# Four sets of expert buffers, and expert rows added to the output by accumulating indirect stores

## The chip, the cores and the metric

The kernel runs on one core of a Trainium2 chip. Its engines work side by side: TensorE (PE in the profile) multiplies, VectorE (DVE), ScalarE (ACT) and GpSimd (POOL) do the elementwise work, SyncE (SP) only issues transfers. Each engine runs its own list of instructions in order and waits on semaphores for the others. The metric is device time in microseconds (us) of one execution.

## The reference

A block of three parts on `x` of 64 sequences by 32 rows by 256 columns, 2048 tokens in all: cross attention to a context of 64 by 257 rows, causal self attention, and a mixture of experts. The change touches the last one.

```
x = x + xattn(layernorm(x), ctx)             # 16 heads, context of 257 rows per sequence
x = x + attn(layernorm(x))                   # causal, 32 rows, ternary weights
xt = layernorm(x)                            # 2048 tokens, 256 columns
probs = softmax(xt @ Wg)                     # 8 experts
eidx, gate = argmax(probs), its probability
pos  = how many earlier tokens chose the same expert
keep = pos < 256                             # an expert takes 256 tokens, the rest are dropped
xd[eidx*256 + pos] = xt                      # only kept tokens
oe = (silu(xd @ W1[e]) * (xd @ W3[e])) @ W2[e]         # 8 experts, hidden 352 (padded to 384)
out = oe[eidx*256 + pos] * gate * keep + (silu(xt @ sw1) * (xt @ sw3)) @ sw2
x = x + out
```

## The kernel before

The tokens are cut into 16 tiles of 128 rows (four sequences). The attention of a tile and the routing of the tile ahead of it are woven: each engine has a written list of steps (`START_ORDER` for the prologue, `ORDER` for a tile), and runs 15 full tiles with it. A 16th pass (`LAST`) runs only the steps named in `LATE`, in the order in which they stand in `ORDER`: the rest of the cross attention of the last four sequences (`pt3`, `o3`, `f`), self attention (`xt1` to `pr`), the second layer norm (`ln2`), the router's logits (`lg`), the shared expert (`up`, `dn`), the position of each token among its expert's tokens (`pos`), and `scat` on POOL, an indirect store of the 128 normalised rows to their slots in `expert_rows` in HBM. In `ORDER` the step `pos` stands behind `up` (on PE behind `dn` too). On DVE `pos` computes three things a token: the slot where it is written (`slot_s`), the slot where its result is read (`slots`), and its gate (`gates`). A tile's output without the experts (`base`) is stored to `out` by SP.

Then come the eight experts. For one expert PE turns the 256 rows (L898, `expert_turn`), does the 12 products of `W1` and `W3` (`expert_up`) and the 6 of `W2` (`expert_down`). A float32 product stands as two records in the trace, so an `up` is x24 and a `down` x12. ACT copies the turned rows (L942), takes the tanh (L1096), copies the result out of the PSUM bank `Db` to one of the two tiles `eo` (which lie in `o_halves`) and stores it to `expert_out` (L1104). DVE makes the hidden values (L1661, L1665). PE's order is skewed: `up` of expert e+1, `turn` of e+2, `down` of e. Weights (`ew13`, `ew2`), rows (`xd`) and `eo` have two sets each. SP asks for expert e+2's `W1`/`W3` (768 KB) and then its rows (256 KB) when PE has finished `up` of expert e, and for its `W2` when PE has finished `down` of e; all go into one queue.

When all eight results are in HBM, POOL gathers, for each of the 16 tiles, the result rows of its tokens (L1259, indirect loads into `got`), DVE multiplies by the gate and adds the base rows that SP has read back from `out` into `fin` (L1678), and SP stores four tiles at a time.

The lines of these steps are L554 to L585 (SP), L892 to L935 (PE), L1091 to L1117 (ACT), L1214 to L1260 (POOL) and L1609 to L1679 (DVE).

## Time and profile before

| | |
|---|---|
| time, median of 3 runs | 1506.91 us (1506.75 to 1508.54) |
| the profiled execution's own time | 1508.46 us |
| its span in the trace | 1506.6 us |
| PE / DVE / ACT / POOL busy | 86% / 66% / 56% / 35% |
| mean granted clock of TensorE | 0.933 of 2.4 GHz |
| tiles 1 to 15 and the prologue end, the last tile begins | about 1322 us |
| first expert's rows are turned on PE | 1385.97 us |
| last expert product ends | 1476.4 us |

Times in the trace run from the span's start; the span leaves 1.9 us of the profiled execution's time outside. A busy share is a mean over stages with different limits: up to about 1322 us PE is nearly full, after it the stages below have limits of their own, and they are read one by one.

### The profile page before, as it was taken

How to read it: one execution, taken by the hardware profiler on the slowest of the kernel's cores; microseconds unless marked ns; L12 is line 12 of the kernel's file. 1: busy time of each engine (PE TensorE's matmuls, PEld its weight loads, DVE VectorE, ACT ScalarE, POOL GpSimd, SP SyncE). 2: the span in 40 equal slices, each digit the busy share in tenths (PEclk: the TensorE clock that was granted, in tenths of full speed). 3: DMA queues.
4: the chain of work that ended last, by engine and by line, in shares of the span. 5: the costliest groups of instructions: out<-in, count | busy, mean ns of one | idle time of the engine just before them, and what ended most of it. 6: DMA issues, size and time to landing. Idle time of an engine off the chain costs nothing.

```text
span 1506.6 us, 35628 instructions
## 1 busy us (share of the span) xinstructions
PE 1297.3 (86%) x10526; PEld 874.2 (58%) x10526; DVE 987.6 (66%) x3748; ACT 837.5 (56%) x3560; POOL 531.6 (35%) x1337
## 2 busy tenths in 40 slices
PE   5877898999999999989898989899999999955881
PEld 2554565666666666665656656566666666634661
DVE  6754777777677777776767676777767777732212
ACT  4445575747475757566566657575747575711110
POOL 2044152525252533435352515252535243310004
PEclk9998999999999999999999999999999999876996
DMA  9000010101010100000000000010101011002344
GB/s 370 31 23 15 9 30 11 32 11 32 11 32 11 33 11 29 11 26 18 22 21 22 21 8 29 11 32 11 32 11 32 11 32 39 31 3 75 120 153 126
DMA packets 41191, 59.65 MB, mean 40 GB/s; under 512 B 5094, under 2 KB 35953, under 8 KB 40096
## 3 DMA queue, kind: packets, MB, share of 16 engines
q1 hardware_dynamic: 36880, 50.73, 10.6%
q0 software_dynamic: 2064, 6.14, 1.2%
q10 hardware_dynamic: 2176, 2.10, 0.4%
q14 instruction: 59, 0.48, 0.1%
q8 instruction: 12, 0.20, 0.1%
HBM read 48.62 MB, written 10.49 MB: 39 GB/s over the span
## 4 chain that ended last, share of the span: by engine, by line
PE 49%; DVE 21%; issue 9%; POOL 8%; DMA 3%; ACT 3%; POOLq 0%; DVEq 0%; SPq 0%; ACTq 0%
PE AB L594 25%; PE Db L594 9%; PE Eb L594 5%; POOL prob L1177 4%; PE C L719 4%; PE C L594 3%; DVE kst L1312 3%; DVE rq L1360 2%; DMA ctxn<-expert_rows 2%; DVE nc_ L1284 2%; DVE nc_ L1285 2%; DVE nb_ L1286 1%; PE C L787 1%; DVE prob L1471 1%; PE C L734 1%
## 5 line engine op out<-in xcount | busy, mean ns | idle before, releaser
L950 ACT ACTIVATE AB<-AB 128x128 f32<-128x128 f32 (+1 forms) x1160 | 305.3, 263 | 172.8 <-PE AB L594 168.3
L1132 POOL TENSOR_TENSOR pjunk<-pjunk 128x1 f32<-128x1 f32 x288 | 56.1, 195 | 748.4 <-DVE sinv L1482 431.3
L1312 DVE BATCH_NORM_STATS2 kst<-AB 128x6 f32<-128x256 f32 x512 | 181.8, 417 | 68.1 <-PE AB L594 63.0
L950 ACT ACTIVATION_READ_ACCUMULATOR AB<-AB 128x1 f32 (+1 forms) x1160 | 217.3, 187 | 0.0
L594 PE MATMUL AB<-wk_hi,c_hi 128*128 128x512 f16 x512 | 203.7, 398 | 11.9 <-DVE smax L1471 2.9
L594 PE MATMUL AB<-wk_lo,c_hi 128*128 128x512 f16 x512 | 201.3, 393 | 0.0
L594 PE MATMUL AB<-wk_hi,c_lo 128*128 128x512 f16 x512 | 199.7, 390 | 0.0
L1020 ACT ACTIVATE prob<-prob,nbias,rq 128x257 f32<-128x257 f32 x256 | 150.6, 592 | 7.9 <-DVE nbias L1477 7.9
L1177 POOL TENSOR_SCALAR prob<-prob,sinv 128x257 f32<-128x257 f32 x256 | 123.4, 482 | 20.2
L594 PE MATMUL AB<-ctxT,qpT 128*128 128x257 f32 x512 | 124.0, 385 | 0.0
L594 PEld LDWEIGHTS AB<-wk_hi,c_hi 128*128 128x128 f16 x512 | 52.2, 102 | 94.7 <-issue 25.2
L594 PE MATMUL Eb<-pT,cn_hi 128*128 128x512 f16 x256 | 88.3, 386 | 14.1 <-DVE o_halves L1492 7.5
L594 PEld LDWEIGHTS AB<-ctxT,qpT 128*128 128x128 f32 x512 | 92.3, 190 | 12.2 <-DVE smax L1471 0.2
L1014 ACT COPY rkb<-C 128x512 f32<-128x512 f32 x128 | 68.6, 591 | 54.2 <-PE C L719 53.3
L1471 DVE CUSTOM_DVE_ANT_0 prob<-AB,rkb 128x257 f32<-128x257 f32 x256 | 95.3, 421 | 0.0
L594 PEld LDWEIGHTS AB<-wk_hi,c_lo 128*128 128x128 f16 x512 | 51.9, 101 | 65.8 <-issue 9.6
L1487 DVE TENSOR_TENSOR pT<-C,pT 128x512 f16<-128x512 f32 x128 | 81.7, 679 | 11.1 <-ACT pT L989 10.4
L594 PE MATMUL Db<-wvo_hi,o_halves 128*128 128x256 f16 x512 | 86.5, 273 | 0.7 <-ACT o_halves L982 0.7
L594 PE MATMUL AB<-x_hi,wqk_hi 128*128 128x128 f16 x512 | 87.0, 219 | 0.0
L594 PE MATMUL AB<-x_lo,wqk_hi 128*128 128x128 f16 x512 | 87.0, 219 | 0.0
L594 PE MATMUL AB<-x_hi,wqk_lo 128*128 128x128 f16 x512 | 86.9, 219 | 0.0
L1492 DVE SCALAR_TENSOR_TENSOR o_halves<-Eb,o_halves 128x512 f16<-128x512 f32 x64 | 44.1, 690 | 64.0 <-ACT o_halves L982 64.0
(252 smaller groups left out, 2923.8 us busy)
## 6 DMA issues: line engine op xcount, KB each, us to landing
ctxT<-in_ctxT SPq DMA_DIRECT2D x64, 128.5 KB, 2.1
ctxn<-in_ctxn SPq DMA_DIRECT2D x64, 128.0 KB, 2.1
wq_hi<-in_w SPq DMA_DIRECT2D x4, 768.0 KB, 5.0
wq_lo<-in_w SPq DMA_DIRECT2D x4, 768.0 KB, 6.3
expert_rows<-base POOLq DMA_DIRECT2D x1, 2048.0 KB, 15.5
xin<-in_x SPq DMA_DIRECT2D x16, 128.0 KB, 2.2
prob<-in_wqT SPq DMA_DIRECT2D x1, 2048.0 KB, 20.4
xres<-in_x SPq DMA_DIRECT2D x16, 128.0 KB, 2.0
```

The costliest lines, as they stand in the source:

```text
L594: return pe.matmul(out, lhsT, rhs, start=start, stop=stop)
L719: ins = pe.transpose(C[:, n, KT * P * (g % 2) + P * tt:KT * P * (g % 2) + P * (tt + 1)], rkx[:, b % 2, tt, P * g:P * (g + 1)], ident)
L950: ins = nc.scalar.activation(k, k, ACT.Square, accum_out=sums[0:m, h:h + 1])
L1014: nc.scalar.copy(rkb[:, b % 2, 2 * n:2 * n + 2, 0:KT * P], C[:, n].rearrange("p (g n) -> p g n", g=2)).then_inc(drained[s].sem, 1)
L1020: ins = nc.scalar.activation(prob[:, b, g], prob[:, b, g], ACT.Exp, bias=nbias[:, b, g:g + 1], scale=rq[:, G * b + g:G * b + g + 1], accum ...
L1132: own.mark(pool.tensor_tensor(pjunk[:, 0:1], pjunk[:, 1:2], pjunk[:, 1:2], ALU.mult))
L1177: ins = pool.tensor_scalar(prob[:, b, g], prob[:, b, g], sinv[:, b, g:g + 1], P_SCALE, ALU.mult, ALU.mult)
L1284: step(V.scalar_tensor_tensor(c, w, -0.5, w, ALU.mult, ALU.mult))
L1312: ins = V.bn_stats(stats[:, 0, 2 * half + n], AB[0:m, 2 + half, 2 * D * n:2 * D * (n + 1)])
L1471: V.tensor_tensor_reduce(prob[:, b, g], AB[:, g, 0:SKV], rkb[:, b % 2, g], 1.0, BELOW, ALU.mult, ALU.max, smax[:, b, g:g + 1]).then_inc(dr ...
L1487: V.tensor_tensor(pT[:, b % 2, 1, tt], C[:, tt], pT[:, b % 2, 0, tt], ALU.subtract).then_inc(drained[s].sem, 1)
L1492: V.scalar_tensor_tensor(o_halves[:, 1, :, rows], Eb[:].rearrange("p (h q) -> p h q", q=SQ), 1.0 / P_SCALE, o_halves[:, 0, :, rows], ALU.m ...
```

## The change

1. Expert weights and rows get four sets instead of two. The new places are tiles that are free by then: `prob`, `wvo_hi`, `wvo_lo` and `qpT`. Weights of experts 2 and 3 are asked for in the last tile, their rows behind those of experts 0 and 1; experts 4 to 7 are asked for when experts 0 to 3 are through `up` and `down`. `eo`, the hidden values and the turned rows keep their number of sets.
2. The gather at the end is gone. A small table in HBM (`mark_rows`, in the place of `expert_out`) gets for each slot two words, the gate and the token's number. It is blanked in the prologue, filled by 16 indirect stores of 128 pieces of 8 bytes (`mark_tokens`), all in the last tile: three behind `n3`, twelve behind `ln1`, one behind `scat`. SP reads it back as `marks` in one transfer. ACT multiplies an expert's result by its slots' gates while copying it out of PSUM, and POOL adds it to `out` by two indirect stores of 128 rows an expert with `compute_op=ALU.add`; a slot without a token has an index out of bounds and is skipped. ACT may write `eo` again only when the stores of two experts earlier have landed.
3. In the prologue DVE works out each token's number for the table: one reduction and 16 small adds, between `ident16` and the split of `wk`, and a memset more.
4. The last tile has its own order (`LAST_ORDER`): `pos` ahead of `up` and `dn` on PE and DVE, `lg` ahead of `up` and `ph3` ahead of `tl3` on ACT.
5. The loops over the experts are written out.

```diff
+SETS = 4
+LAST_ORDER = {
+    "PE": "pt3 o3 f xt1 qkv qk sc pv st pr xt2 lg pos up dn".split(),
+    "ACT": "ph3 tl3 oh3 xt1 qkv qk sc pv xt2 lg up".split(),
+    "DVE": "dp3 do3 f qkv sc sm ys yv pr ln2 lg pos up dn".split(),
+    "POOL": "n3 mk0 ln1 mk1 y ln2 scat mk3".split(),
+}
...
@@ SP
+            for e in (0, 1):
+                load_up(e)
+                load_down(e)
+            store_base(p)
+            sp.wait_ge(filled["5"].sem, filled["5"].at(p, "pt2"))
+            load_up(2)
+            load_down(2)
+            sp.wait_ge(filled["D"].sem, filled["D"].at(LAST, "f"))
+            load_up(3)
+            load_down(3)
+            sp.wait_ge(scattered.sem, scattered.at(LAST, "scat"))
+            load_rows(0)
+            load_rows(1)
+            store_base(LAST)
+            sp.wait_ge(marked, 16 * TILES)
+            sp.dma_start(marks[:].rearrange("p e a two -> p (e a) two"), mark_rows.rearrange("(n p) two -> p n two", p=P))\
+                .then_inc(marks_in, 16)
+            load_rows(2)
+            load_rows(3)
+            for e in range(SETS, E):
+                p, k = Period("expert", (e - SETS) // 2), e % 2
+                sp.wait_ge(filled["2"].sem, filled["2"].at(p, f"h{k}"))
+                load_up(e)
+                load_rows(e)
+                sp.wait_ge(filled["D"].sem, filled["D"].at(p, f"dn{k}"))
+                load_down(e)
...
@@ ACT
-                act.wait_ge(oe_out[k].sem, oe_out[k].before(p))
-                drain(p, f"dn{k}", "D", flat2(eo[k]), Db[:])
-                act.wait_ge(drained["D"].sem, drained["D"].at(p, f"dn{k}"))
-                act.dma_start(oe_rows[bass.ds(i * (2 * CAP) + k * CAP, CAP), :].rearrange("(a p) c -> p a c", p=P), eo[k])\
-                    .then_inc(oe_out[k].sem, 16)
+                act.wait_ge(marks_in, 16)
+                if e >= 2:
+                    for a in range(2):
+                        act.wait_ge(res_out[k][a], 16 * (e // 2))
+                act.wait_ge(filled["D"].sem, filled["D"].at(p, f"dn{k}"))
+                for a in range(2):
+                    ins = nc.scalar.activation(eo[k][:, a], Db[:, DIM * a:DIM * (a + 1)], ACT.Copy, scale=marks[:, e, a, 0:1])
+                ins.then_inc(drained["D"].sem, 1)
...
@@ POOL
+            def mark_tokens(tiles):
+                if TILES - 1 not in tiles:
+                    pool.wait_ge(slot_ready.sem, slot_ready.before(LAST))
+                    pool.wait_ge(marks_blank, 16)
+                gate()
+                for n in tiles:
+                    pool.indirect_dma_start(mark_rows, bass.IndirectOffsetOnAxis(ap=slots[:, n:n + 1], axis=0), tile_marks[:, n], None,
+                                            bounds_check=E * CAP - 1, oob_is_err=False).then_inc(marked, 16)
...
-            for n in range(TILES):
-                pool.indirect_dma_start(got[n], None, oe_rows, bass.IndirectOffsetOnAxis(ap=slots[:, n:n + 1], axis=0))\
-                    .then_inc(gathered[n], 16)
+            pool.wait_ge(base_out.sem, base_out.at(LAST, "o"))
+            for e in range(E):
+                p, k = Period("expert", e // 2), e % 2
+                pool.wait_ge(drained["D"].sem, drained["D"].at(p, f"dn{k}"))
+                for a in range(2):
+                    pool.indirect_dma_start(d["out"], bass.IndirectOffsetOnAxis(ap=marks[:, e, a, 1:2].bitcast(U32), axis=0),
+                                            eo[k][:, a], None, bounds_check=TOKENS - 1, oob_is_err=False,
+                                            compute_op=ALU.add).then_inc(res_out[k][a], 16)
...
@@ DVE
+                step(V.tensor_reduce(token[:], tri, AX.X, ALU.add, negate=True))
+                for n in range(TILES):
+                    V.tensor_scalar(tile_marks[:, n, 1:2].bitcast(U32), token[:], float(P * n + P - 1), None, ALU.add)
...
-                here = fin[n // 4][:, n % 4]
-                V.scalar_tensor_tensor(here, got[n], gates[:, n:n + 1], here, ALU.mult, ALU.add)\
-                    .then_inc(res_ready, 1)
```

PE before, from the router's logits of the last tile (`wg`) to the first experts; `sw` is the shared expert, `onehot` and `seen` are the step `pos`:

```order
L594 MATMUL Db<-wg,xn2T 128x8 x2
L594 MATMUL C<-xn2T,sw 128x128 x12
L594 MATMUL Eb<-sw,hT 128x256 x3
L594 MATMUL Db<-onehot,consts_sb 128x8
L594 MATMUL Db<-seen,ones 128x8
L898 MATMUL Eb<-consts_sb,ctxn 128x128 x4
L594 MATMUL AB<-rkb,wq_hi 128x256 x12
L898 MATMUL Eb<-consts_sb,ctxn 128x128 x4
```

PE in the changed kernel at the same place:

```order
L614 MATMUL Db<-wg,xn2T 128x8 x2
L614 MATMUL Db<-onehot,consts_sb 128x8
L614 MATMUL Db<-seen,ones 128x8
L614 MATMUL C<-xn2T,sw 128x128 x12
L614 MATMUL Eb<-sw,hT 128x256 x3
L919 MATMUL Eb<-consts_sb,ctxn 128x128 x4
L614 MATMUL AB<-rkb,wq_hi 128x256 x12
L919 MATMUL Eb<-consts_sb,ctxn 128x128 x4
```

The two small products of `pos` moved ahead of the 15 products of the shared expert.

POOL before, from the last step `n3` (it ends with `plast`) to the end of the program:

```order
L1187 TENSOR_TENSOR plast<-prob,plast 128x4
L1152 TENSOR_TENSOR rstd<-var,minus_half 128x1 x3
L1132 TENSOR_TENSOR pjunk<-pjunk 128x1
L1218 DMA expert_rows<-xn,slot_s 2048x256
L1259 DMA pxT<-expert_out,slots 128x256 x8
L1259 DMA px<-expert_out,slots 128x256 x8
```

POOL in the changed kernel, the same stretch; `rstd` three times is `ln1`, `y` and `ln2`, `expert_out` now holds the table:

```order
L1199 TENSOR_TENSOR plast<-prob,plast 128x4
L1144 TENSOR_TENSOR pjunk<-pjunk 128x1
L1240 DMA expert_out<-tile_marks,slots 2048x2 x3
L1164 TENSOR_TENSOR rstd<-var,minus_half 128x1
L1144 TENSOR_TENSOR pjunk<-pjunk 128x1
L1240 DMA expert_out<-tile_marks,slots 2048x2 x12
L1164 TENSOR_TENSOR rstd<-var,minus_half 128x1 x2
L1144 TENSOR_TENSOR pjunk<-pjunk 128x1
L1230 DMA expert_rows<-xn,slot_s 2048x256
L1144 TENSOR_TENSOR pjunk<-pjunk 128x1
L1240 DMA expert_out<-tile_marks,slots 2048x2
L1286 DMA out<-o_halves,marks 2048x256 x16
```

Sixteen indirect stores stand between and behind the three `rstd`, and the 16 gathers at the end became 16 accumulating stores, two for each expert.

## Rows read from the trace of the kernel before

**Rows 1.** Waits, 1384 to 1480 us (total us, times, longest us).

```profile
PE Eb L898 <- DMA ctxn<-expert_rows: 20.5, 6, 7.2
```

**Rows 2.** PE in order of time, experts (start us, us, instructions, [idle before]).

```profile
1385.97 1.11 PE L898 MATMUL Eb<-consts_sb,ctxn 128*128 128x128 f32 x4 [7.19 <-DMA ctxn<-expert_rows]
1387.81 7.57 PE L594 MATMUL AB<-rkb,wq_hi 128*128 128x256 f32 x24 [0.72 <-issue]
1395.21 0.60 PE L898 MATMUL Eb<-consts_sb,ctxn 128*128 128x128 f32 x4
1396.57 5.44 PE L594 MATMUL AB<-rkb,wq_lo 128*128 128x256 f32 x24 [0.76 <-ACT rkb L942]
1401.85 0.60 PE L898 MATMUL Eb<-consts_sb,ctxn 128*128 128x128 f32 x4
...
1404.88 5.34 PE L594 MATMUL AB<-rkb,wq_hi 128*128 128x256 f32 x24
1413.60 1.12 PE L898 MATMUL Eb<-consts_sb,ctxn 128*128 128x128 f32 x4 [3.38 <-DMA ctxn<-expert_rows]
1414.51 5.21 PE L594 MATMUL Db<-wqk_lo,pT 128*128 128x256 f32 x12
...
1464.84 5.34 PE L594 MATMUL AB<-rkb,wq_lo 128*128 128x256 f32 x24
...
1473.59 2.83 PE L594 MATMUL Db<-wqk_lo,pT 128*128 128x256 f32 x12 [0.82 <-ACT o_halves L942]
```

**Rows 3.** Windows: length, PE, PEld, DVE, ACT, POOL busy, clock, DMA share, GB/s.

```profile
32.00:40.00 8.00, 5.17 (x13) 1.88 (x14) 7.62 (x24) 1.27 (x9) 0.00 (x0) 0.60 1.03 390
...
1376.00:1380.00 4.00, 2.06 (x12) 1.66 (x10) 1.89 (x12) 0.00 (x0) 0.00 (x1) 1.00 0.05 18
...
1384.00:1388.00 4.00, 1.31 (x5) 0.94 (x6) 0.00 (x0) 0.58 (x1) 0.00 (x0) 0.50 0.79 229
```

**Rows 4.** In order of time, the last tile's end, all engines.

```profile
1363.58 0.55 POOL L1152 TENSOR_TENSOR rstd<-var,minus_half 128x1 f32<-128x1 f32 x1 [24.87 <-DVE var L1572]
...
1371.54 4.62 PE L594 MATMUL C<-xn2T,sw 128*128 128x128 f32 x24
...
1372.85 0.23 DVE L1597 TENSOR_SCALAR onehot<-consts_sb,eidx 128x8 f32<-128x8 f32 x1
...
1378.41 0.37 PE L594 MATMUL Db<-seen,ones 128*128 128x8 f32 x2
...
1378.82 0.17 DVE L1613 CUSTOM_DVE_ANT_0 posx<-Db,onehot 128x8 f32<-128x8 f32 x1
...
1379.77 0.15 DVE L1624 TENSOR_TENSOR slot_s<-flat,lmax 128x1 uint32<-128x1 f32 x1
...
1380.73 1.11 POOL L1218 DMA_INDIRECT expert_rows<-xn,slot_s  x1 [0.54 <-issue]
1383.19 0.91 SPq L556 DMA_DIRECT2D ctxn<-expert_rows  x2
```

**Rows 5.** In order of time, the last tile's beginning.

```profile
1326.29 0.57 ACT L942 CAST pTl<-Db 12x512 f16<-12x512 f32 x1 [3.50 <-PE Db L594]
...
1327.48 0.59 PE L594 MATMUL Eb<-pT,cn_hi 128*128 128x512 f16 x1 [1.23 <-ACT pT L989]
...
1338.14 0.57 POOL L1152 TENSOR_TENSOR rstd<-var,minus_half 128x1 f32<-128x1 f32 x1 [13.36 <-DVE var L1297]
```

**Rows 6.** In order of time, the end of the program.

```profile
1476.51 0.58 ACT L942 COPY o_halves<-Db 128x512 f32<-128x512 f32 x1 [3.06 <-PE Db L594]
...
1480.13 1.00 POOL L1259 DMA_INDIRECT pxT<-expert_out,slots  x1 [98.29 <-DMA expert_out<-o_halves]
1481.44 0.96 POOL L1259 DMA_INDIRECT pxT<-expert_out,slots  x1 [0.30 <-issue]
...
1498.95 0.95 POOL L1259 DMA_INDIRECT px<-expert_out,slots  x1 [0.30 <-issue]
```

**Rows 7.** In order of time, PE's first product of the prologue.

```profile
12.08 0.61 PE L594 MATMUL AB<-wk_hi,y 128*64 128x512 f16 x1 [12.08 <-DVE wk_lo L1412]
```

More of the change, by code:

```diff
@@ L57 @@
 N_CONST = sum(CONSTS.values())
-DVE_STEPS = dict(pro=78, full=85, last=37, expert=0)
-POOL_STEPS = dict(pro=37, full=40, last=5, expert=0)
+DVE_STEPS = dict(pro=79, full=85, last=37, expert=0)
+POOL_STEPS = dict(pro=37, full=40, last=8, expert=0)
 class Period:
@@ L174, in steps_of @@
         return START_ORDER[engine]
+    if p.kind == "last" and engine in LAST_ORDER:
+        return LAST_ORDER[engine]
     return [s for s in ORDER[engine] if p.kind == "full" or s in LATE]
@@ L317, in build @@
         slots = sb("slots", [P, TILES], U32)
-        gates = sb("gates", [P, TILES])
+        tile_marks = sb("tile_marks", [P, TILES, 2])
+        token = sb("token", [P, 1])
+        marks = sb("marks", [P, E, 2, 2])
+        no_marks = sb("no_marks", [P, E * CAP // P, 2])
         sig = sb("sig", [P, FC, P])
@@ L572, in _ @@
-            with sp.Fori(0, E // 2 - 1) as i:
-                p = Period("expert", i)
-                for k in range(2):
-                    sp.wait_ge(filled["2"].sem, filled["2"].at(p, f"h{k}"))
-                    load_up(i * 2 + (2 + k), k)
-                    load_rows(i * 2 + (2 + k), k)
-                    sp.wait_ge(filled["D"].sem, filled["D"].at(p, f"dn{k}"))
-                    load_down(i * 2 + (2 + k), k)
-            for n in range(4):
-                sp.wait_ge(res_ready, 4 * n + 4)
-                sp.dma_start(d["out"][4 * n * P:4 * (n + 1) * P, :].rearrange("(a p) c -> p a c", p=P),
-                             fin[n]).then_inc(res_out, 16)
@@ L997, in wqk_high @@
                     .then_inc(hi_ready.sem, 1)
-            for k in range(2):
-                act.sem_inc(oe_out[k].sem, 16)
             def step_tw(p):
@@ L1238, in _ @@
                      "ln2": lambda p: rsqrt(p, "ln2", 3), "scat": scatter,
+                     "mk0": lambda p: mark_tokens(range(0, 3)), "mk1": lambda p: mark_tokens(range(3, TILES - 1)),
+                     "mk3": lambda p: mark_tokens([TILES - 1]),
                      "hl": step_hl, "rkl": step_rkl, "cl": split_last}
@@ L1364, in _ @@
             own.enter(PRO)
-            for tile_, value in ((zeros, 0.0), (ones, 1.0), (minus_half, -0.5), (seen, 0.0),
+            for tile_, value in ((zeros, 0.0), (ones, 1.0), (no_marks, NO_TOKEN), (minus_half, -0.5), (seen, 0.0),
                                  (heads, 0.0), (vals, 0.0), (plast, 0.0), (pTl, 0.0), (cl_rows, 0.0)):
```

165 lines of the change are left out of this document (70 added, 95 removed).

## The prediction, made before the changed kernel was run

> **What bounds the kernel now.** I read the engines' shares first, then the chain of waits over the last 250 us, the order of time from 1320 us to the end, and the windows for the clock. The page's mean PE share, 86%, belongs to the tiles; the change leaves these nearly as they are. What it touches are four stretches with other limits.
>
> In the experts PE is the engine that others wait for, and PE itself waits for rows: 20.5 us in 6 waits [rows 1]. 7.2 of them are the wait for the first rows, after the last slot is known. The other five, 13.3 us, come because an expert's rows stand in SP's queue behind 768 KB of weights of the same expert and are asked for only two experts ahead. Where rows are there, as between the third turn at 1401.85 and the third `up` at 1404.88 [rows 2], PE has no gap to speak of. The clock makes the waits dearer: PE had 1.00 of 2.4 GHz at 1376 to 1380 us, idled, and had 0.50 (1.2 GHz) at 1384 to 1388 [rows 3]. The first `up` then took 7.57 us where later ones take 5.34, and a `down` behind a wait took 5.21 where the last took 2.83 [rows 2].
>
> Before the experts a serial chain runs from the router to the first rows: one-hot, position, slot, store, load [rows 4]. After them the end is POOL's: 16 gathers, the first at 1480.13, the last at 1498.95, 1.25 us apart [rows 6]. PE's last product ended at 1476.4 [rows 2], so 30.2 us of the span of 1506.6 are tail.
>
> **The parts, with their sum.** All against the profiled execution.
>
> *Prologue, +1.7.* DVE's step `low` gets a reduction over 128 columns and 16 adds on one column, ahead of the split of `wk`; PE's first product waits for that split at 12.08 [rows 7]. From the first row of `pos` to `slot_s` DVE goes through nine such small instructions in 0.95 us, 0.106 each [rows 4], so 16 take 1.7; pipelined better they take 1.3, the reduction adds perhaps 0.3. I take 1.7. Later DVE is busy 7.62 of 8 us at 32 to 40 us [rows 3], so I count it as passed on in full. Bounds: 0, if the waits for weights there swallow it, and 2.7. The memset and the blanking of the table (one transfer nobody waits for until the last tile) cost nothing; cover for POOL's issue is PE's wait for DVE until 12.08.
>
> *`ph3` ahead of `tl3`, -1.0.* At the last tile's start ACT casts `pTl` (1326.29, 0.57 us) before `pT`, for which PE waits until 1327.48 [rows 5]. The `pT` banks are full before `Db` is, so up to 1.2 us go; at least 0.57 do, unless PE is then late for another half. I take 1.0.
>
> *Marks in the last tile, 0.* `mk0` issues three indirect stores and `mk1` twelve. Nearest rows: gathers follow each other every 1.25 us, the scatter takes 1.11 us to issue [rows 4, 6]. `mk0` then takes about 4.5 us with its gate, inside POOL's idle time of 13.36 us before `ln1` [rows 5]; `mk1` 12 x 1.25 + 0.7 = 15.7 us inside the 24.87 us before `y` [rows 4]. Behind the waiting POOL stand `y`, `ln2` and the scatter, and DVE and PE wait for each, so a thirteenth microsecond too many would go straight to the end: the point is 2.0 us a store. What nothing here shows is a store of pieces of 8 bytes. Lower bound 0, upper the rival below.
>
> In a sentence of its own: the Trainium skill, in DMA: Bandwidth & Descriptors (Specifications), says that pieces under 512 bytes make the transfer read, modify and write; no run here shows such pieces alone, and by that rule the table's stores could only be dearer than the 1 KB ones, which is the direction of that rival.
>
> *`pos` ahead of `up` and `dn`, -4.8.* The one-hot is ready at 1372.85 + 0.23 = 1373.08. PE's two small products ended at 1378.78 because 15 larger ones stood before them; now they may start at 1373.1 and, at half clock, end about 1373.95 instead of 1378.78 [rows 4]. Everything behind moves with them: slot at 1375.1 for 1379.92, scatter 1375.9 for 1380.73, SP's rows 1378.4 for 1383.19, first turn 1381.2 for 1385.97 [rows 2, 4]. PE's shared expert is moved back by 2.4 us: its products start at 1373.95 for 1371.54, and its last ends near 1380.9 by the same spacing, just ahead of the rows. So both are late at about the same time, and more than 4.8 is not to be had here. `mk3` adds 1.25 us on POOL behind the scatter, where nobody but the table waits.
>
> *First `turn` and `up` at full clock, -2.6.* PE now idles some 0.3 us before the first turn, not 7.19. From turn 1 to turn 2 took 9.24 us; with a row pair at full clock it is 1.36 (1395.21 to 1396.57) + 5.28 (to 1401.85) = 6.64 [rows 2]. Bounds: 0 and 2.6.
>
> *The experts, -18.2.* Rows 2 and 3 are asked for before the first product, the rest four experts ahead, so a period is 3.03 (turn to next `up`, 1401.85 to 1404.88) + 5.28 = 8.31 us. From the second turn: 6.64 + 5 x 8.31 + 3.03 + (1464.84 to the end 1476.42) 11.58 + 0.2 for two activations instead of one copy of `Db` = 63.0, against 81.2 in the trace [rows 2]. The check: 13.3 us of waits and nearly 5 us of half clock behind them. ACT and DVE have room in a period of 8.31. The stores, two an expert, need POOL for 2.5 us of 8.31, if one costs what a gather does.
>
> *The tail, -23.2.* From the last product: ACT 0.1 + 0.7 (two of 256 columns; one of 512 took 0.58), POOL's start 0.6 (the scatter's issue wait 0.54), the second store 1.25 later, landing 4.0, span end 0.3: 7.0 against 30.2 [rows 4, 6]. The scatter landed in 2.46 [rows 4]; the accumulating store also has to read `out`, and I take 4.0, bounds 2.5 and 8. POOL's price for issuing an accumulating store is nowhere in the trace: the nearest rows say 1.25, and I take that.
>
> The Trainium skill (DMA: Bandwidth & Descriptors, Rules for kernel authors) says an accumulate reads its destination and writes later, and under Latency gives about 0.8 us as the least HBM round trip; by that estimate a store lands after 2.46 + 0.8 = 3.3 us, and the sum is 0.7 lower.
>
> Sum: +1.7 - 1.0 - 4.8 - 2.6 - 18.2 - 23.2 = -48.1. Span 1458.5, the execution's own time 1508.46 - 48.1 = 1460.4. The median lies 1.55 under the profiled execution, so the prediction is **1458.8 us**.
>
> **Rivals.**
> *The table comes back late.* SP reads it as 2048 pieces of 8 bytes, and rows 2 and 3 stand behind it in the queue. Asked for at about 1382; the rows of experts 0 and 1, 512 pieces of 1 KB, had the first landing 2.8 us after issue (1383.19 to 1385.97) [rows 2, 4]. By the number of pieces the table could take 4 x 2.8 = 11 us or more; the third turn needs its rows at 1381.2 + 13.3 = 1394.5, so up to 12.5 us are free. At 20 us it would cost 7.5, and half clock behind it 2: 1468. For it: the piece count; against: the slack. 10%.
>
> *The mark stores hold POOL.* Past 2.0 us each, `y` is late. At 3 us: 12 x 3 + 0.7 - 24.9 = +11.8, so 1471 [rows 4]. Against: a gather has as many pieces and issues in 1.25. 7%.
>
> *The stores pace the experts.* `eo` has still two tiles: ACT waits for the stores of expert e-2 before it frees `Db`, and with ACT the tanh of the next expert stands, and PE. Two stores may take 8.31 us, 4.15 each. At 5 us each the run is theirs: the first store can start at 1381.2 + 17.2 = 1398.4, plus 0.7 for the earlier terms, 16 x 5 and 4.3 at the end give 1483. 10% for 4.2 to 6.4 us.
>
> *The same mechanism, on the other side.* The end passes 1506.6 when 1399.1 + 16 c + 4.3 does: from c = 6.45 us a store the kernel is slower than before; at 8 us it is 1531. For it speaks that no accumulating transfer is in the trace at all, and that they work on random rows of HBM; against, that a scatter of the same rows lands in 2.46 us [rows 4], and c would have to be over twice that. 5%.
>
> *The change doesn't do what it says.* PE still waits for rows, because weights of four experts share the queue, and only tail and `pos` gain: 1458.8 + 18.2 + 2 = 1479. Against: they are asked for 33 us ahead. 3%.
>
> **How the numbers follow.** The forecast has 65%, and its own range is 1452 to 1466: prologue 0 to 2.7, `ph3` 0 to 1.2, clock 0 to 2.6, landing 2.5 to 8, and some microseconds for code that is now written out instead of looped. The table late 10% (1462 to 1470), marks 7% (1465 to 1475), paced stores 10% (1466 to 1506), slow stores 5%, waits kept 3%. The range 1452 to 1478 holds the forecast and most of the first two rivals, and some of the third: 8 in 10. Faster by over 0.2% (about 3 us, what a measurement here can tell from no change) 94%, the same 1%, slower 5%.
>
> **What would show it.** Right: first turn on PE near 1382; no wait of PE for rows from then on; clock 1.00 throughout the experts; eight periods of 8.3 us; last product near 1451.5; two stores behind it, the end 7 us later; `rstd` of `y` not late. Wrong: POOL's accumulating stores more than 1.25 us apart, ACT's copies of `Db` released by a transfer instead of by PE, a third turn late behind the table, or POOL's `y` released by POOL itself. The forecast falls if the stores cost over 4.15 us each or the mark stores over 2.0.

## The result, and the profile after

| | before | changed kernel |
|---|---|---|
| median | 1506.83 us (1506.39 to 1508.54, 4 runs) | 1461.76 us (1457.33 to 1465.12, 4 runs) |
| profiled execution, its own time | 1508.46 us | 1458.61 us |
| its span | 1506.6 us | 1456.6 us |
| mean granted clock | 0.933 | 0.949 |

The ratio is 0.9697, 95% interval 0.9663 to 0.9731. In a second comparison the changed kernel had 1464.39 us (1462.32 to 1466.68, 4 runs) and 0.9707 (0.9681 to 0.9733). The forecast was 1458.8, with 1452 to 1466 as its own range.

The waits of the experts, total us, times, longest; this line answers to [rows 1]:

```profile
PE Eb L919 <- DMA ctxn<-expert_rows: 2.2, 1, 2.2
```

20.5 us in six waits have become 2.2 in one, and that one is the wait for the very first rows (3.1 in a second trace of the changed kernel). PE in order of time, in the places of [rows 2]:

```profile
1376.14 0.66 PE L919 MATMUL Eb<-consts_sb,ctxn 128*128 128x128 f32 x4 [2.22 <-DMA ctxn<-expert_rows]
1377.52 7.10 PE L614 MATMUL AB<-rkb,wq_hi 128*128 128x256 f32 x24 [0.72 <-issue]
1384.46 0.60 PE L919 MATMUL Eb<-consts_sb,ctxn 128*128 128x128 f32 x4
1385.79 5.42 PE L614 MATMUL AB<-rkb,wq_lo 128*128 128x256 f32 x24 [0.72 <-issue]
1391.04 0.60 PE L919 MATMUL Eb<-consts_sb,qpT 128*128 128x128 f32 x4
...
1394.07 5.34 PE L614 MATMUL AB<-rkb,prob 128*128 128x256 f32 x24
1399.25 0.60 PE L919 MATMUL Eb<-consts_sb,qpT 128*128 128x128 f32 x4
...
1444.15 2.83 PE L614 MATMUL Db<-wvo_lo,pT 128*128 128x256 f32 x12 [1.10 <-ACT o_halves L1123]
```

From the third turn at 1391.04 to the fourth at 1399.25 pass 8.21 us. Each later turn follows at that distance with no bracket behind it: the engine was never idle ahead of it. But the first `up` still takes 7.10 us instead of 5.3 to 5.4. The windows say why (length, PE, PEld, DVE, ACT, POOL busy, clock, DMA share, GB/s); they are the places of [rows 3] and those around the first turn:

```profile
1370.00:1372.00 2.00, 1.64 (x8) 1.35 (x7) 0.45 (x2) 0.00 (x0) 0.67 (x1) 0.60 0.46 31
1372.00:1374.00 2.00, 1.56 (x6) 1.06 (x6) 0.35 (x2) 0.00 (x0) 0.00 (x0) 1.00 0.81 134
1374.00:1376.00 2.00, 0.00 (x0) 0.00 (x0) 0.38 (x1) 0.00 (x0) 0.00 (x0) 1.00 0.47 136
1376.00:1378.00 2.00, 1.14 (x6) 0.91 (x7) 0.00 (x0) 0.58 (x1) 0.00 (x0) 1.00 0.84 68
1378.00:1380.00 2.00, 2.00 (x7) 1.61 (x7) 0.00 (x0) 0.00 (x0) 0.00 (x0) 0.60 0.79 241
1380.00:1382.00 2.00, 2.00 (x6) 1.59 (x6) 0.00 (x0) 0.00 (x0) 0.00 (x0) 0.54 0.00 0
...
1388.00:1446.00 58.00, 56.90 (x276) 49.81 (x275) 13.36 (x14) 15.05 (x27) 19.82 (x13) 1.00 0.49 114
```

PE stood idle in 1374 to 1376, and its clock then went to 0.60 and 0.54 until 1382. From 1388 to 1446 PE is busy 98% at 1.00 (2.4 GHz). The DMA columns hold something not foreseen: 46% busy at 31 GB/s in 1370 to 1372, 84% at 68 GB/s in 1376 to 1378. Pieces of 8 bytes were under way in both stretches: those of the last mark store in the first, those of the table on its way back in the second (2073 of the 2190 packets there are under 512 bytes). The last tile's end in order of time, all engines, answers to [rows 4]:

```profile
1355.74 0.57 POOL L1164 TENSOR_TENSOR rstd<-var,minus_half 128x1 f32<-128x1 f32 x1 [10.92 <-DVE var L1603]
...
1365.02 0.23 DVE L1628 TENSOR_SCALAR onehot<-consts_sb,eidx 128x8 f32<-128x8 f32 x1
...
1367.31 0.15 DVE L1655 TENSOR_TENSOR slot_s<-flat,lmax 128x1 uint32<-128x1 f32 x1
...
1368.25 1.03 POOL L1230 DMA_INDIRECT expert_rows<-xn,slot_s  x1 [0.52 <-issue]
...
1369.68 0.99 POOL L1240 DMA_INDIRECT expert_out<-tile_marks,slots  x1 [0.16 <-issue]
1370.62 0.90 SPq L572 DMA_DIRECT2D ctxn<-expert_rows  x2
...
1374.81 0.43 SPq L591 DMA_DIRECT2D marks<-expert_out  x1
```

POOL's `rstd` of `y` still had 10.92 us to spare: the marks did not hold it. The slot comes 2.29 us after the one-hot, where it came 6.92 after it. But SP asked for the first rows at 1370.62 and PE got them at 1376.14, 5.5 us later instead of 2.8, with the last tile's mark store (`mk3`, 1369.68) just ahead. The transfers, issue to landing, in the stretch 1369 to 1377:

```profile
ctxn<-expert_rows SPq DMA_DIRECT2D x2, 256.0 KB, 5.6
...
marks<-expert_out SPq DMA_DIRECT2D x1, 16.0 KB, 3.2
```

The table came back in 3.2 us and nobody waited for it. In the same stretch before, two such row loads took 2.9. The end of the program, in the place of [rows 6]:

```profile
1443.17 0.84 ACT L1123 ACTIVATE o_halves<-Db,marks 128x256 f32<-128x256 f32 x2 [4.45 <-PE Db L614]
...
1444.78 1.55 POOL L1286 DMA_INDIRECT out<-o_halves,marks  x1 [4.37 <-ACT o_halves L1123]
...
1447.10 0.84 ACT L1123 ACTIVATE o_halves<-Db,marks 128x256 f32<-128x256 f32 x2 [3.09 <-PE Db L614]
1448.71 1.55 POOL L1286 DMA_INDIRECT out<-o_halves,marks  x1 [0.53 <-issue]
1450.56 1.54 POOL L1286 DMA_INDIRECT out<-o_halves,marks  x1 [0.30 <-issue]
```

An accumulating store is issued in 1.55 us, 1.85 from one to the next, where a gather needed 1.25. Expert 6's second (at 1446.63) is still being issued when expert 7's result is there at 1447.94. The last product ends at 1446.98, so the tail is 9.6 us instead of 30.2. And the prologue's first product, answering to [rows 7], with the row of the adds ahead of it:

```profile
6.84 1.06 DVE L1433 TENSOR_SCALAR tile_marks<-token 128x1 uint32<-128x1 f32 x16
...
12.93 0.61 PE L614 MATMUL AB<-wk_hi,y 128*64 128x512 f16 x1 [12.93 <-DVE wk_lo L1443]
```

Where the 50.0 us between the two spans went, by milestones (`x` is the output of the cross attention, one a tile):

| stretch | before | after | difference | predicted |
|---|---|---|---|---|
| start to the first `x` | 147.3 | 143.8 | -3.5 | +1.7 |
| first to 15th `x` | 1112.8 | 1110.1 | -2.7 | 0 |
| 15th to last `x` | 76.64 | 73.54 | -3.1 | -1.0 |
| last `x` to `slot_s` | 43.0 | 39.9 | -3.1 | -4.8 |
| `slot_s` to the first turn | 6.2 | 8.8 | +2.6 | 0 |
| first turn to the second | 9.24 | 8.32 | -0.9 | -2.6 |
| second turn to the last product's end | 81.2 | 62.5 | -18.7 | -18.2 |
| last product's end to the end | 30.2 | 9.6 | -20.6 | -23.2 |

The sum is near the forecast's -48.1, but the terms are not all right: 10.0 us more than foreseen came in the first three rows, and 8.6 less in the four rows on `slot_s`, the first turn and the tail. Executions of one kernel differ by some microseconds in the first two rows (in the traces of the changed kernel's second run and of the kernel before alike, a stretch at half clock stands at about 34 us that the trace above has not: first `x` at 148.7 and 147.3), so these two rows are not read for one pair. The third row has a part of the clock in it as well: the mean granted clock of that stretch is 0.91 before and 0.95 after.

### The profile page after: what moved, and what is told of

Same layout as the page of the kernel before. It is cut to its first block, busy times and chain, and to the rows that moved or that the text cites. A ratio compares the mean times of both kernels' runs of the same rounds, so it can differ in the third digit from the quotient of the medians.

```text
span 1456.6 us, 35544 instructions
## 1 busy us (share of the span) xinstructions
PE 1286.4 (88%) x10526; PEld 868.3 (60%) x10526; DVE 982.2 (67%) x3750; ACT 839.7 (58%) x3568; POOL 558.5 (38%) x1357
## 3 DMA queue, kind: packets, MB, share of 16 engines
HBM read 44.44 MB, written 8.42 MB: 36 GB/s over the span
## 4 chain that ended last, share of the span: by engine, by line
PE 51%; DVE 21%; issue 9%; POOL 7%; ACT 3%; DMA 1%; POOLq 1%; DVEq 0%; ACTq 0%
PE AB L614 27%; PE Db L614 8%; PE Eb L614 6%; PE C L739 4%; POOL prob L1189 4%; PE C L614 3%; DVE kst L1340 3%; DVE rq L1388 2%; DVE nc_ L1312 2%; DVE nc_ L1313 2%; DVE nb_ L1314 1%; DVE prob L1502 1%; PE C L754 1%; PE C L807 1%; DVE px L1598 1%
```

## The experiments

**The changed kernel again.** No edit; it shows how far two comparisons agree and gives a second trace.

> The changed kernel again, to see how its executions spread: so far 1457.3, 1458.6, 1464.9 and 1465.1 us. If the two groups come from TensorE's clock before the last tile, an execution near 1465 has a granted mean near 0.944 and tiles 1 to 15 some 5 us longer than the 1110.1 us of the profiled one; the experts are then the same, first turn to last product 71 us. If they come from the stores at the end, the tiles agree within 1 us and the end is longer.

1464.39 us, ratio 0.9707. The profiled execution took 1466.7 us, 8.1 more than the first one. Neither of the two sources looked for holds these 8.1 us: the tiles took 1110.1 us again, and the tail is 9.6 us again. 4.9 lie ahead of the first `x` (148.7 for 143.8), 1.9 between the last `x` and the first turn, 1.3 between the first two turns (9.58 for 8.32; the first `up` took 8.12 us behind a wait of 3.10). With both traces at half clock in the same stretch of the prologue the first `x` came at 148.7 against 147.3 before: +1.4, near the +1.7 of the sum. The other traces below bear this out: where the mean clock up to the first `x` is 0.91, it comes at 147.1 and 147.3 in the two kernels without the 16 adds and at 148.4 and 148.7 in two with them; with the adds it comes at 146.5 to 146.9 where the clock is 0.92 and at 143.6 to 144.7 where it is 0.93. But from the last `x` to the one-hot, which the change does not touch on PE, DVE or ACT, it took 39.6 us where before took 36.1 and the first trace of the changed kernel 37.6. That is taken up below.

**Two sets instead of four.** Experts 0 and 1 loaded as before, the rest asked for two experts ahead; the accumulating stores stay.

```diff
-SETS = 4
+SETS = 2
...
-            load_up(2)
-            load_down(2)
...
-            load_up(3)
-            load_down(3)
...
-            load_rows(2)
-            load_rows(3)
```

> The changed kernel with SETS = 2: weights and rows of expert e+2 asked for, weights first, when expert e is through up, and no early loads of experts 2 and 3. Theory, the sets are worth what I summed for the experts: five or six waits of PE for rows of 2 to 3.4 us come back with half clock behind one or two of them, 15 to 18 us, 1477 to 1480. Rival, those waits came from the other traffic of the old end (the read-back of 2 MB of base rows, the result stores): under 4 us, at most 1466.

**Two sets, rows asked for ahead of the weights.**

```diff
+                load_rows(e)
                 load_up(e)
-                load_rows(e)
```

> The same with SETS = 2, but SP asks for the rows ahead of the weights. Theory, rows were late only because 768 KB stood before them in the queue: 256 KB land in 3 to 4 us, the turn comes 6.6 us after the asking and the weights are needed 8 us after it, so nearly all waits go, and two sets are as good as four within 3 us, near 1463. Rival, two sets are too few for the bytes: the wait moves to the weights (PE's up released by a transfer), and the time stays over 1470.

The first has 1475.47 us (0.9785, 0.9756 to 0.9814), the second 1463.99 (0.9713, 0.9684 to 0.9743), which cannot be told from four sets in the same comparison (1464.39, 0.9707). The waits, of the first, then of the second:

```profile
PE Eb L911 <- DMA ctxn<-expert_rows: 11.5, 6, 3.0
```

```profile
PE Eb L911 <- DMA ctxn<-expert_rows: 3.6, 2, 3.0
```

So the waits came from the order in SP's queue, 768 KB of weights ahead of 256 KB of rows, as the first paragraph of the prediction read them. Four sets remove them, and so does a swap of two lines with half the memory. Two sets with the old order now lose 8.5 us in five waits (11.5 less the first's 3.0) and not 13.3 as before. In time that is 11 us more than with four sets, between the 15 to 18 of the theory and the under 4 of the rival. From the second turn to the last product's end it took 73.8 us, with the lines swapped 63.3, with four sets 62.5, and 81.2 in the kernel before. So 11.3 of the 18.7 us hang on the queue, by more sets or by its order. The other 7.4 came with the rest of the change; the result stores and the 2 MB of base rows read back, which shared the DMA engines with the loads before, are a likely reason, but no run takes them apart.

**Stores that replace instead of adding.** The rows of kept tokens get the expert's part alone: the shared expert and the residual are left out there.

```diff
-                                            eo[k][:, a], None, bounds_check=TOKENS - 1, oob_is_err=False,
-                                            compute_op=ALU.add).then_inc(res_out[k][a], 16)
+                                            eo[k][:, a], None, bounds_check=TOKENS - 1, oob_is_err=False).then_inc(res_out[k][a], 16)
```

> The 16 stores of the expert rows without the addition: the rows of the experts overwrite the output, so shared expert and residual are lost for kept tokens. Theory, the addition costs issue time (1.55 us with it, 0.95 to 1.1 as the scatter and the gathers have) and landing: stores 1.3 us apart, the end 6.0 us after the last store's start becomes 4 to 5, and with four stores in a row at the end the tail of 9.6 us shrinks to 6.5 to 7.5. Rival, the issue time is the same for any store in this place: 1.85 us apart still, and the end within 1 us.

1463.24 us, 0.9705 (0.9679 to 0.9731): the time is that of the changed kernel's 1464.39 within what can be told. POOL's last store:

```profile
1456.44 0.97 POOL L1286 DMA_INDIRECT out<-o_halves,marks  x1 [0.30 <-issue]
```

Without the addition a store takes 0.97 us to issue and the next follows 1.27 later. The trace's last product ended at 1453.4 and its span at 1461.8: a tail of 8.4 (6.5 to 7.5 was expected), 5.4 of it behind the last store's start, where the adding one has 9.6 and 6.0. The stores landed 2.4 us after issue, the adding ones (the second line):

```profile
out<-o_halves,marks POOLq DMA_INDIRECT x16, 2.4
```

```profile
out<-o_halves,marks POOLq DMA_INDIRECT x16, 3.8
```

So the addition costs 0.57 us an issue, 1.4 to the landing (medians of sixteen) and 1.2 us of the tail. What it costs the first seven experts lies beside PE's work.

**The last mark store behind the first rows.** POOL waits for rows 0 and 1 before `mk3`; SP asks for rows 2 and 3 ahead of the table.

```diff
+                if TILES - 1 in tiles:
+                    for k in range(2):
+                        pool.wait_ge(xd_in[k], 16)
...
+            load_rows(2)
+            load_rows(3)
             sp.wait_ge(marked, 16 * TILES)
...
-            load_rows(2)
-            load_rows(3)
```

> The changed kernel, but POOL stores the last tile's marks only when the rows of experts 0 and 1 have landed, and SP asks for rows 2 and 3 ahead of the table. Theory: the 128 pieces of 8 bytes of that store hold the 16 transfer engines just when the first rows are asked for (their landing took 5.5 us, before the change 2.8); with them away PE's wait before the first turn, 2.2 us in one execution and 3.1 in another, falls under 0.7, the clock has less of a gap to fall in, and the time is 2 to 5 us lower, 1459 to 1462. Rival: the rows are slow because SP's two loads come right behind the scatter, whatever POOL does after it; the wait stays over 2 us, the time within 1.5.

1459.21 us, 0.9696 (0.9669 to 0.9723). The rows and the first `up`, in order of time:

```profile
1373.45 0.90 SPq L572 DMA_DIRECT2D ctxn<-expert_rows  x2
...
1376.48 0.63 PE L919 MATMUL Eb<-consts_sb,ctxn 128*128 128x128 f32 x4 [0.60 <-DVE base L1663]
```

The same transfer in the stretch 1366 to 1378:

```profile
ctxn<-expert_rows SPq DMA_DIRECT2D x2, 256.0 KB, 2.9
```

The landing is back at 2.9 from 5.6 (the table, also moved, is no cause of the first rows' delay: in the changed kernel it is asked for at 1374.81, when rows asked for at 1370.62 would have been there by 1373.5), the wait is 0.60 us, with the rows and DVE's `base` there at about the same time, and the first `up` takes 5.42 instead of 7.10. So 128 pieces of 8 bytes, 1 KB in all, had held up the first rows by 2.7 us, and without the longer wait there was no half clock. The wait alone does not settle the clock: in the kernel before, PE ran at 1.00 behind waits of 2.61, 2.55 and 2.29 us (the first is shown, a `down` at full speed behind it), and at half clock behind 3.38 and, from about 1450 on, behind 2.44.

```profile
1427.51 0.65 PE L898 MATMUL Eb<-consts_sb,ctxn 128*128 128x128 f32 x4 [2.61 <-DMA ctxn<-expert_rows]
1428.00 2.76 PE L594 MATMUL Db<-wqk_hi,pT 128*128 128x256 f32 x12
```

The trace shows the delay of the rows and its end; the ratio's interval overlaps the changed kernel's.

**Two halves of an expert's result, each with its own bank.** On top of the last one: the columns of the first 128 rows go to `Db`, those of the second to `C`, and ACT and POOL take each half as it is ready.

```diff
-                        ins = mm(Db[:, DIM * a:DIM * (a + 1)], ...
+                        ins = mm((Db[:, 0:DIM], C[:, 0, 0:DIM])[a], ...
+                    if a == 0:
+                        ins.then_inc(half_down, 1)
...
-                act.wait_ge(filled["D"].sem, filled["D"].at(p, f"dn{k}"))
+                act.wait_ge(half_down, e + 1)
...
-                pool.wait_ge(drained["D"].sem, drained["D"].at(p, f"dn{k}"))
+                pool.wait_ge(half_out, e + 1)
```

> The same, and each half of an expert's result (128 rows) goes its own way: the second half's products are written to another PSUM bank, ACT copies the first half while PE works on the second, and POOL stores it at once. Theory, the tail is POOL's: four stores 1.85 us apart from the seventh result on, so a start 2 us earlier takes 2 us off the end: tail after the last product 7.5 instead of 9.6 us, time 1457 to 1460. Rival, the end is the landing of the last store, which waits for its expert's second half anyway: tail 9 us or more, as e_mk3_late.

1458.27 us, 0.9672 (0.9649 to 0.9694). The last product ended at 1450.33 and the span at 1458.7: a tail of 8.4 for 9.6 (7.5 was expected, 9 or more by the rival). The stores are still 1.85 to 1.95 apart; what was won is that the last begins 2.25 us behind the last product, not 3.6.

**`pos` behind the shared expert again.** The changed kernel with the old place of `pos` and `lg`.

```diff
-    "PE": "pt3 o3 f xt1 qkv qk sc pv st pr xt2 lg pos up dn".split(),
-    "ACT": "ph3 tl3 oh3 xt1 qkv qk sc pv xt2 lg up".split(),
-    "DVE": "dp3 do3 f qkv sc sm ys yv pr ln2 lg pos up dn".split(),
+    "PE": "pt3 o3 f xt1 qkv qk sc pv st pr xt2 lg up dn pos".split(),
+    "ACT": "ph3 tl3 oh3 xt1 qkv qk sc pv xt2 up lg".split(),
+    "DVE": "dp3 do3 f qkv sc sm ys yv pr ln2 lg up dn pos".split(),
```

> The changed kernel with pos behind up and dn again in the last tile (PE, DVE) and lg behind up on ACT. Theory, the earlier slots are worth what the chain says: last slot 4.6 us later against the router's one-hot, first turn 4 to 5 us later, and a longer gap on PE keeps the first up at half clock, 4 to 6 us in all, 1468 to 1470. Rival, the gain was already given back by the wait for rows and PE's own later shared expert: under 2 us.

1467.74 us, 0.9745 (0.9726 to 0.9764). The rows in order of time:

```profile
1367.30 0.23 DVE L1628 TENSOR_SCALAR onehot<-consts_sb,eidx 128x8 f32<-128x8 f32 x1
...
1375.06 0.15 DVE L1655 TENSOR_TENSOR slot_s<-flat,lmax 128x1 uint32<-128x1 f32 x1
...
1383.90 1.12 PE L919 MATMUL Eb<-consts_sb,ctxn 128*128 128x128 f32 x4 [9.83 <-DMA ctxn<-expert_rows]
```

One-hot to slot is 7.76 us instead of 2.29: the order is worth 5.5 where it acts (4.8 predicted), and PE waits 9.83 us for rows instead of 2.22. From the last `x` to the first turn it took 56.4 us, against 48.7 and 50.6 in the two traces of the changed kernel.

**The kernel before with the new order alone.** `LAST_ORDER` and nothing else of the change.

```diff
+LAST_ORDER = {
+    "PE": "pt3 o3 f xt1 qkv qk sc pv st pr xt2 lg pos up dn".split(),
+    "ACT": "ph3 tl3 oh3 xt1 qkv qk sc pv xt2 lg up".split(),
+    "DVE": "dp3 do3 f qkv sc sm ys yv pr ln2 lg pos up dn".split(),
+}
```

> The kernel before with nothing changed but the last tile's order (ph3 ahead of tl3, lg and pos ahead of up and dn). No mark stores are there. Theory, all of the last tile's gain without what the marks take back: last tile's start to its x 1 us shorter, first turn 4.8 us earlier against the one-hot, first up near 5.5 us instead of 7.57: 6 to 8 us under the kernel before, 1501 to 1503. Rival, the clock's stretches before the last tile decide the first, and the first up stays slow: 3 to 5 us.

1502.6 us (1497.7 to 1506.1, 10 runs), 0.9972 (0.9958 to 0.9987), 4.2 us. SP and PE in order of time:

```profile
1378.09 0.35 SPq L500 DMA_DIRECT2D out<-base  x1
1378.48 0.98 SPq L565 DMA_DIRECT2D ctxn<-expert_rows  x2
...
1381.31 0.97 PE L907 MATMUL Eb<-consts_sb,ctxn 128*128 128x128 f32 x4 [3.71 <-DMA ctxn<-expert_rows]
```

Here SP stores the last tile's base rows ahead of the loads, and base is now late, behind `up` and `dn`. So the rows are asked for at 1378.48, long after the slots are written, and part of the gain stays there: from the last `x` to the first turn it took 47.9 us for 49.2, and the first `up` took 8.05 us, where 5.5 was expected. The changed kernel has rows ahead of the base store on SP. The order and SP's swap belong together. The last interval between two `x` is 73.51 us, as in the changed kernel, so marks and weight loads have no part in it; how `ph3` ahead of `tl3` and the clock share it is taken up further down.

**Where the last tile's extra time comes from.** From the last `x` to the one-hot:

| kernel | us |
|---|---|
| before, the new order alone, before with the token numbers | 36.1, 35.8, 35.5 |
| changed kernel, two traces | 37.6, 39.6 |
| last mark late, halves on top, `pos` behind | 39.6, 40.1, 39.8 |
| two sets, two sets swapped, stores without the addition | 39.2, 39.8, 39.6 |

PE in the changed kernel's second trace, the 128 small products of the self attention, 16 us after `x`; the kernel with the new order alone has them in one row of 1.53 us:

```profile
1348.34 0.66 PE L614 MATMUL AB<-wt_q 16*32 16x32 f32 x38 [0.72 <-issue]
1349.39 0.26 PE L614 MATMUL AB<-wt_q 16*32 16x32 f32 x1 [0.39 <-issue]
1350.79 0.32 PE L614 MATMUL AB<-wt_q 16*32 16x32 f32 x3 [1.14 <-issue]
1351.50 1.13 PE L614 MATMUL AB<-wt_q 16*32 16x32 f32 x86 [0.39 <-issue]
```

DVE's next instruction stood 7.03 us idle for them, 4.27 where they are in one piece.

```profile
1352.62 0.88 DVE L1578 TENSOR_TENSOR sc<-AB,consts_sb 128x128 f32<-128x128 f32 x4 [7.03 <-PE AB L614]
```

The DMA view of 1345 to 1357, packets, MB and the time they took as a share of 16 engines, for this kernel and then for the new order alone:

```profile
q8 instruction: 1, 0.02, 1.6%
```

```profile
q8 instruction: 1, 0.02, 0.5%
```

One piece of 16 KB of instructions took 12 x 16 x 0.016 = 3.1 us there and 1.0 here. What else was under way was `mk1`, whose last stores are issued at 1347.47 and 1348.74. Experiment: seven stores in `mk0` and eight in `mk1`, so that the last is issued before that fetch.

```diff
-                     "mk0": lambda p: mark_tokens(range(0, 3)), "mk1": lambda p: mark_tokens(range(3, TILES - 1)),
+                     "mk0": lambda p: mark_tokens(range(0, 7)), "mk1": lambda p: mark_tokens(range(7, TILES - 1)),
```

> The changed kernel with seven instead of three mark stores in mk0 and eight instead of twelve in mk1. In the changed kernel's second profiled run the last tile went from its x to its one-hot in 39.6 us, in the first in 37.6, in the kernel before in 36.1; the 128 small products of the self attention, 16 us after x, stood in pieces with gaps of 0.39 to 1.14 us, and a 16 KB piece of instructions fetched there took 3.1 us of a DMA engine's time instead of 1.0. Theory (8-byte stores that still run then slow that fetch): with eight stores mk1 issues its last at about +12.5 us, before the fetch at about +16, so the products stand in one piece, the fetch takes about 1 us, the one-hot comes 36 to 37 us after x, and the median is 1 to 3 us under the changed kernel (1459 to 1462). Rival (the extra time is code or execution scatter, not the stores): the gaps stay, 37.6 to 39.7 us, median 1461 to 1465. Second rival: the four stores moved to mk0 slow another fetch there, and f is later by as much.

In order of time:

```profile
1351.60 1.53 PE L614 MATMUL AB<-wt_q 16*32 16x32 f32 x128 [0.72 <-ACT wt_q L958]
...
1353.12 0.88 DVE L1578 TENSOR_TENSOR sc<-AB,consts_sb 128x128 f32<-128x128 f32 x4 [4.27 <-PE AB L614]
...
1372.11 0.23 DVE L1628 TENSOR_SCALAR onehot<-consts_sb,eidx 128x8 f32<-128x8 f32 x1
```

The products are in one row of 1.53 us, DVE's wait is 4.27 again, and the one-hot comes 36.5 us after `x` (1335.57), 3.1 less than in the second trace of the changed kernel and 1.1 less than in the first. The fetch's share over 1328 to 1366 is 0.2% (1.2 us), against 0.5% (3.0 us) over a stretch as long in that second trace. As to the mechanism the theory stands, and the other traces agree: with twelve stores in `mk1` (eight traces) the fetch has 0.6 to 0.7% of 1330 to 1360, 2.9 to 3.4 us, and with eight stores or none (four traces) 0.2 to 0.3%, 1.0 to 1.4 us. In seven of the eight the products stand in pieces and DVE waits 6.96 to 8.42 us. In the eighth, the first trace of the changed kernel, they stand in one row of 1.89 us and DVE waits 4.62, so there only 0.4 us of the delay lie at these products. The time does not show it: 1463.40 us (1458.18 to 1466.84, 6 runs), 0.9713 (0.9688 to 0.9737). In its trace the last `x` is 3.3 us later than in the second one of the changed kernel. 2.4 of it lie in the tiles, which the edit does not touch. 1.0 lies in the last interval (74.61 for 73.57 us), where the four moved stores are. That looks like the second rival, but the mean clock there is 0.93 for 0.95, two kernels with three stores in `mk0` took 73.9 and 74.1 us at 0.93, and the last experiment, with seven, took 73.7 at 0.95. At most some tenths are left for the moved stores.

**The token numbers alone.** The kernel before with the reduction and the 16 adds in step `low`.

```diff
...
+                step(V.tensor_reduce(token[:], tri, AX.X, ALU.add, negate=True))
+                for n in range(TILES):
+                    V.tensor_scalar(tile_marks[:, n, 1:2].bitcast(U32), token[:], float(P * n + P - 1), None, ALU.add)
```

> The kernel before with the reduction and the 16 small adds of the token numbers ahead of the split of wk, and nothing else of the change. Prediction's term: +1.7 us, passed on in full; the matched pair of traces says +1.4. By that 1508.2 to 1508.6 where the kernel before has 1506.9, PE's first product at 12.9 instead of 12.1 and the first tile's x 1.4 to 1.7 later at equal clock. Rival (a later wait of the prologue swallows it): no change, first x at 147.3.

1508.75 us (1504.47 to 1513.34, 12 runs), 1.0013 (0.9996 to 1.0031): between -0.6 and +4.7 us. PE's first product came at 13.71 instead of 12.08, but the first `x` at 146.7, not later than before's 147.3, with a shorter stretch at half clock. The delay of the first product is shown, and one of 1.1 to 1.6 us at the first `x` by the pairs at equal clock given above; how much of it reaches the end stays open.

**All of it.** The halves, the late last mark, seven marks in `mk0`, and the token numbers at a place of the prologue where DVE waits for ACT.

```diff
-    "DVE": """low wk KL ... tw s0 s1 i0 K6 dp0
+    "DVE": """low wk KL ... tw s0 s1 tok i0 K6 dp0
...
+            def step_tok(p):
+                step(V.tensor_reduce(token[:], tri, AX.X, ALU.add, negate=True))
+                for n in range(TILES):
+                    V.tensor_scalar(tile_marks[:, n, 1:2].bitcast(U32), token[:], float(P * n + P - 1), None, ALU.add)
```

> Table's last mark behind the first rows, an expert's two result halves released one by one, seven marks in mk0, and the token numbers worked out in DVE's idle time at about 84 us of the prologue instead of ahead of wk. The parts should add: against the changed kernel -3.5 (first turn's wait and the half clock of the first up), -1.2 (tail), -1 to -3 (fetch), and PE's first product at 12.1 instead of 12.9 with the prologue 1.4 to 1.7 shorter. Expected 1453 to 1457. Rival: the prologue's part and the fetch's part are taken up by waits further on: 1458, as with the first two parts alone.

1455.52 us (1454.99 to 1457.79, 5 runs), 0.9668 (0.9645 to 0.9692), the lowest median of all. In order of time:

```profile
12.07 0.61 PE L616 MATMUL AB<-wk_hi,y 128*64 128x512 f16 x1 [12.07 <-DVE wk_lo L1458]
...
1375.87 0.66 PE L921 MATMUL Eb<-consts_sb,ctxn 128*128 128x128 f32 x4 [0.60 <-DMA ctxn<-expert_rows]
```

From the last `x` (1330.97) to the first turn pass 44.9 us; before took 49.2, the changed kernel 48.7 and 50.6 in its two traces. So the 4.8 us of the sum can be had (4.3 measured), once the 8-byte stores are out of the way of the fetch and of the rows. The prologue's part is not shown: PE's first product came at 12.07, as before, but the first `x` at 150.0, later than in any other trace, at a mean clock of 0.89 up to there; the 15 tiles then took 1107.3 us for 1110.1. Of the ratio only the distance to the changed kernel's first two comparisons can be named, 0.9697 and 0.9707, and the intervals overlap; the 0.9672 of the halves cannot be told from it.

## Why the prediction was right

The time and the main mechanisms were right. Term by term:

- **Experts, -18.2.** -18.7 in the trace. Periods of 8.21 us for 8.31, no wait from the second turn on, clock 1.00. The two-set experiments show that the reading of the queue was right, and that the cause is its order more than the number of sets. They account for 11.3 of the 18.7 us; the other 7.4, which the prediction put down to the same queue, were gained with two sets and weights ahead of rows as well.
- **Tail, -23.2.** -20.6; the term was mis-sized by 2.6. From the last product's end to the first of the two stores it was 1.7 us for 1.4; the second came 1.85 later for 1.25, since the price of issuing an accumulating store, for which the gather's stood, is half as much again; and from its start to the end it was 6.0 where 4.0 + 0.3 were taken. The landing itself, 3.8 in the median, was sized well; what follows it until the span ends is about 2 us, not 0.3.
- **`pos` ahead, -4.8.** The chain from one-hot to slot got 4.6 shorter in the trace (6.92 to 2.29); the experiment that puts it back made it 5.5 longer. The step that failed is the one that "Marks in the last tile, 0" stands for. Costed as POOL's time alone, which was right (0.97 us a store, `rstd` of `y` with 10.92 us to spare), it left out what the pieces do to others: +2.7 us to the landing of the first rows, shown by taking `mk3` out of their way, and +1.1 to 3.1 us between the last `x` and the one-hot, shown by moving four stores out of `mk1` (36.5 us for 37.6 and 39.6), up to 2.8 of it at the small products that waited for PE's instruction fetch. The 0.5 us that are left over against the kernel before are not explained. From `x` to the first turn the changed kernel gained 0.5 us in one trace and lost 1.4 in the other.
- **First `up` at full clock, -2.6.** -0.9, since the wait stayed at 2.22 us and the half clock with it; in the second trace, with a wait of 3.10, it was +0.3. Without the wait it came: 5.42 us.
- **Prologue, +1.7.** +1.1 to +1.6 between traces of equal clock. The reduction and the adds put off DVE's next instruction by 1.3 us (6.52 to 7.82), the adds alone took 1.06 where 1.7 was counted; PE's first product came 0.7 to 1.7 later over ten traces. In the time it is not to be told from zero.
- **`ph3` ahead, -1.0.** The last interval went from 76.64 to 73.54, but its mean clock from 0.91 to 0.95. At 0.93 the old order has 75.42 us (in the kernel with the token numbers) and the new one 73.9, 74.1 and 74.6 (halves, two sets swapped, seven marks in `mk0`). So 0.8 to 1.5 are the order's, about what was forecast, and the rest of the 3.1 goes with the clock.

The rivals. The table was back in 3.2 us, against a fear of 11 to 20: a count of pieces says little of how long 2048 of them take when they are read in one transfer. The mark stores did not hold POOL. The stores did not pace the experts: 1.85 us each, far from 4.15, POOL idle 4.37 us ahead of a pair. The slower side, from 6.45 us a store, was never near. One of the prediction's own signs of being wrong did come true: the accumulating stores were more than 1.25 us apart. It cost part of the 2.6 by which the tail fell short and nothing more, since the stores of the first seven experts lie beside PE's work.

The Trainium skill, in DMA: Bandwidth & Descriptors (Specifications), has pieces under 512 bytes read, modified and written. That they could only be dearer is borne out on the DMA engines and not at the issuing engine: 8-byte pieces were issued in 0.97 us, no more than rows of 1 KB. Whether reading and writing back is the reason no run shows. The estimate that the prediction drew from the Trainium skill's least HBM round trip (DMA: Bandwidth & Descriptors, Latency and other measured facts), 3.3 us to the landing of an accumulating store, came out 0.5 short: the trace has 3.8. Against the plain store that is 1.4 more, 0.6 of it the longer issue, so the 0.8 us left over are as long as that round trip; that they are one, no run shows.

That the first profiled execution gained 50.0 us where 48.1 were forecast (1458.6 us for its 1460.4) is in part luck: 10.0 us more than foreseen came in rows that vary with the clock, and 8.6 less in the last tile, the first turn and the tail. The second profiled execution took 1466.7 us. The medians of 1461.8 and 1464.4 are the fairer comparison, 3.0 and 5.6 us off.

Open: whether it is the size of the pieces or any indirect store that slows a fetch (only 8-byte ones were moved), what brought the 7.4 us of the experts that do not hang on the queue, and how the prologue's delay is shared out.

## What to carry to other kernels

When a consumer waits for a small transfer, look first at what stands ahead of it in its queue: two lines swapped did what two more sets of buffers did. Cost a store of tiny pieces twice, once on the engine that issues it and once on the DMA engines, against every load and instruction fetch that falls within it, and put it where nobody waits for either. Here a gather at the end was well replaced by stores beside the work, even at half as much again an issue, since only the last ones counted. And compare stretches between two traces only at equal granted clock: the first `x` of one and the same kernel came anywhere between 143.8 and 148.7 us.

## What the runs showed of the hardware

- 128 pieces of 8 bytes made a load of 256 KB behind them land in 5.6 us instead of 2.9, and with the last of twelve such stores under way a 16 KB instruction fetch took 3.1 us instead of 1.0.
- 2048 pieces of 8 bytes, read in one transfer, landed in 3.2 us; the DMA engines were 84% busy at 68 GB/s meanwhile.
- An indirect store of 128 rows of 1 KB issues in 0.97 us, with the addition in 1.55; landing had a median of 2.4 and 3.8 us over the sixteen.
- Behind one wait of 2.22 us the clock stood at 0.54 to 0.60, behind one of 0.60 us in the same place the next `up` ran at full speed; behind waits of 2.29 to 2.61 us elsewhere the clock stayed at 1.00.
